# Values of pairs 4 to 15 from seven block products in place of eight, in an attention and feed-forward kernel

## What is computed

```python
def attention(x, Wq, bq, Wk, bk, Wv, bv, Wo, bo, gq, gk):
    q = rms_norm(x @ Wq + bq, gq)      # the norm runs over all 4096 columns
    k = rms_norm(x @ Wk + bk, gk)
    v = x @ Wv + bv                    # [1024 tokens, 4096]: 32 heads of 128
    attn = softmax(q @ k.T / sqrt(128))  # for each batch and head
    return (attn @ v) @ Wo + bo
x = x + layernorm(attention(layernorm(x), ...))
x = x + layernorm(ffn(layernorm(x), ...))
```

## Time and profile before

| | us |
|---|---|
| median of 3 runs | 1073.78 |
| lowest and highest | 1073.11, 1077.03 |
| span of the profiled execution | 1069.7 |

### The profile page before, as it was taken

One profiled execution on the slowest core, in us unless ns is written; L12 is line 12 of the kernel. 1 busy time (PEld: TensorE's weight loads), 2 busy tenths in 40 slices (PEclk: granted clock), 3 DMA queues, 4 the chain that ended last, 5 costly groups with the idle time before them and its releaser, 6 DMA issues.

```text
span 1069.7 us, 20038 instructions
## 1 busy us (share of the span) xinstructions
PE 1052.9 (98%) x5781; PEld 563.7 (53%) x5781; DVE 789.6 (74%) x1831; ACT 741.3 (69%) x1470; POOL 681.1 (64%) x597
## 2 busy tenths in 40 slices
PE   7999999999999999999999999999999999999997
PEld 4444444444445655555555555555555555555454
DVE  8767766666645887777777777777777777778887
ACT  4666766666656787676777767677776767777756
POOL 2667767676657476676666667666666766666713
PEclk9999999999999999999999999999999999999999
DMA  6688985656663679977676776767677676765702
GB/s 240 175 237 261 269 232 194 223 215 222 203 142 135 199 187 267 227 173 177 177 184 165 189 179 165 176 178 187 162 190 179 163 176 180 189 163 128 175 33 79
DMA packets 312072, 197.76 MB, mean 185 GB/s; under 512 B 275424, under 2 KB 279392, under 8 KB 312032
## 3 DMA queue, kind: packets, MB, share of 16 engines
q1 hardware_dynamic: 304400, 193.71, 65.5%
q10 hardware_dynamic: 7632, 3.57, 1.5%
HBM read 94.45 MB, written 35.68 MB: 122 GB/s over the span
## 4 chain that ended last, share of the span: by engine, by line
PE 91%; DVE 5%; ACT 2%; DMA 1%; issue 1%; SPq 0%; POOL 0%; DVEq 0%; ACTq 0%
PE ps L1236 30%; PE ps L1237 30%; PE ps L1238 30%; DMA wa_stage<-w_qk 1%; DVE pair_q L2061 1%; ACT ps L1031 0%; DVE ps L2047 0%; DVE stats L1630 0%; DMA pair_k<-pair_q 0%; ACT xh L1024 0%; ACT pair_q L1040 0%; PE ps L1348 0%; DVE y L2011 0%; DVE wa_lo L1735 0%; DVE y L2172 0%
## 5 line engine op out<-in xcount | busy, mean ns | idle before, releaser
L2047 DVE TENSOR_SCALAR_CACHE_REDUCE ps<-ps,score_down 128x512 f32<-128x512 f32 x256 | 177.5, 756 | 88.6 <-PE ps L1238 87.9
L2061 DVE SCALAR_TENSOR_TENSOR pair_q<-ps,row_inv,pair_q 128x512 f16<-128x512 f32 x256 | 174.5, 744 | 54.7 <-ACT pair_q L1040 54.6
L1031 ACT ACTIVATE ps<-ps,neg_max 128x512 f32<-128x512 f32 x256 | 168.2, 657 | 44.9 <-DVE ps L2047 44.9
L1236 PE MATMUL ps<-xh,wa_hi 128*128 128x512 f16 x512 | 194.3, 379 | 1.8 <-DVE wa_lo L1735 1.8
L1237 PE MATMUL ps<-xl,wa_hi 128*128 128x512 f16 x512 | 194.3, 379 | 0.0
L1238 PE MATMUL ps<-xh,wa_lo 128*128 128x512 f16 x512 | 194.3, 379 | 0.0
L1040 ACT ACTIVATE pair_q<-ps,row_inv 128x512 f16<-128x512 f32 x256 | 154.9, 688 | 21.5 <-DVE row_inv L2054 21.5
L758 POOL CAST oth<-o_t 128x512 f16<-128x512 f32 x62 | 37.8, 609 | 201.0 <-ACT o_t L1005 200.9
L664 POOL TENSOR_TENSOR acc<-acc,squares 128x512 f32<-128x512 f32 x120 | 151.1, 1281 | 1.7 <-ACT squares L882 1.7
L1237 PE MATMUL ps<-wv_lo,xh 128*128 128x256 f16 x512 | 139.7, 273 | 0.0
L1236 PE MATMUL ps<-wv_hi,xh 128*128 128x256 f16 x512 | 139.7, 273 | 0.0
(11 more groups left out here) (236 smaller groups left out, 2220.9 us busy)
## 6 DMA issues: line engine op xcount, KB each, us to landing
q_k_scratch<-qk_out SPq DMA_DIRECT2D x64, 512.0 KB, 3.9
qk_in<-q_k_scratch SPq DMA_DIRECT2D x64, 512.0 KB, 3.4
wa_stage<-w_qk SPq DMA_DIRECT2D x32, 512.0 KB, 4.8
u_stage<-w_vo SPq DMA_DIRECT2D x32, 512.0 KB, 5.5
wv_stage<-w_vo SPq DMA_DIRECT2D x16, 512.0 KB, 4.2
wo_stage<-w_vo SPq DMA_DIRECT2D x16, 512.0 KB, 4.4
qk_tops<-qk_top_scratch ACTq DMA_DIRECT2D x27, 128.0 KB, 4.2
y<-x SPq DMA_DIRECT2D x8, 256.0 KB, 5.4
```

What stands on the lines that cost most here:

```text
L1031: act.activation(ps[:, SCORE + i, :], ps[:, SCORE + i, :], ACT.Exp, bias=neg_max[:, sl, i:i + 1], scale=-1.0, accum_out=row_sum[:, sl, i:i ...
L1236: pe.matmul(outp, lhs[0], rhs[0], start=first, stop=False)
L2047: dve.tensor_scalar(ps[:, SCORE + i, :], ps[:, SCORE + i, :], score_down[:, sl, i:i + 1], None, ALU.mult, ALU.min, accum_out=neg_max[:, sl ...
L2061: dve.scalar_tensor_tensor(out=pair_q[:, 1, i, :], in0=ps[:, SCORE + i, :], scalar=row_inv[:, sl, i:i + 1], in1=pair_q[:, 0, i, :], op0=AL ...
```

## The change

For pairs 4 to 15, two pairs and two token tiles are taken as a 2 by 2 block product over the two halves of the 512 inner numbers: tiles t and t + 2, inner halves, and the two pairs' weights (256 columns each). Eight block products give the four results before; the new kernel forms seven (Strassen's scheme in Winograd's form: C, A, E, B, D, G, F), each two inner chunks of three matmuls of 256 columns. There are 24 groups of seven (`gi`): 6 double pairs, 4 tiles each (g). A group takes two steps. The step that begins one has products C and A behind `scores`, and E and B behind `attend`; the step that ends one has D and G behind `scores` and F behind `attend`. Steps 11 to 58 carry them. Steps 11 to 14 also still form values of pair 3 as before, into bank 7; steps 59 to 62 form none.

The partial sums share one bank: `WORK` and `ROOT` are the two halves of bank 6. ScalarE keeps a scaled C (`save_c`), copies ROOT over WORK three times a group (`copy_root`) and takes the second pair's high halves (`high_second`); VectorE adds for the first pair (`first_sums`) and takes the second pair's low halves (`low_second`); GpSimd splits the sums (`split_sums`). Sums of x are formed once on GpSimd in phase A (36 instructions); sums of weights, five for each double pair, on GpSimd, with seven high halves on ScalarE (`high_w`) and seven low halves on GpSimd (`low_w`). SP loads both pairs' weights at once (`load_both`) in place of `load_wv`. `wv` splits of pairs 4 to 15 fall away. The feed-forward weights, whose staging place the new loads use, are loaded and measured (`largest_of_base`) in pair 13 and no longer in pair 1. GpSimd's scaling of a weight has a second multiplication, by 1.0. Several semaphores are merged into `begun`.

```diff
-        X_UP, W_UP, QK_UP, P_UP = 2.0 ** 10, 2.0 ** 14, 2.0 ** 9, 2.0 ** 14
+        X_UP, W_UP, QK_UP, P_UP = 2.0 ** 9, 2.0 ** 14, 2.0 ** 9, 2.0 ** 14
...
+            def load_both(b):
+                for k, part in enumerate((first_w, second_w)):
+                    sp.dma_start(part, w_vo[bass.ds(2 * b + 4 + k, 1)].rearrange(
+                        "a p (h n) -> p (a h) n", h=2)).then_inc(f_loaded, 16)
...
+            with sp.Fori(1, FORMED) as c:
+                for j in range(8):
+                    step(2 * c + j // 4, j % 4)
+                    if j == 4:
+                        sp.wait_ge(w_low_ready, PARTS * c)
+                        load_both(c)
...
+            def form_x(dst, src, other, op):
+                pool.wait_ge(x_formed, x_forms[0])
+                x_forms[0] += 1
+                pool.tensor_tensor(dst, src, other, op).then_inc(x_formed, 1)
...
+            phase_a(1, high_a)
+            phase_a(2, low_a)
+            phase_a(3, both_halves)
+            phase_a(4, split_a)
+            phase_a(5, high_e)
+            phase_a(6, low_e)
+            phase_a(7, split_e)
+            phase_a(8, high_d)
+            phase_a(9, low_d)
+            phase_a(10, split_d)
+            phase_a(11, high_g)
+            phase_a(12, low_g)
+            phase_a(13, both_halves)
+            phase_a(14, split_g)
...
+            def low_w(b, k):
+                pool.wait_ge(w_high_ready, PARTS * b + k + 1)
+                pool.tensor_tensor(flat(w_low(k)), w_source(k), flat(w_high(k)),
+                                   ALU.subtract).then_inc(w_low_ready, 1)
...
+            def split_sums(g, gi):
+                tiles = slice(first_tile(g), first_tile(g) + 3, 2)
+                pool.wait_ge(q_sum_ready, 2 * gi + 2)
+                pool.sem_inc(begun, 1)
+                pool.tensor_copy(vh[:, tiles, :], v_s).then_inc(q_cast_ready, 1)
+                pool.wait_ge(q_cast_ready, gi + 1)
+                pool.tensor_tensor(vl[:, tiles, :], v_s, vh[:, tiles, :], ALU.subtract).then_inc(q_rest_ready, 1)
...
+            def building(c, j):
+                def some():
+                    if j == 0:
+                        form_g(c - 1)
+                    if j == 1:
+                        low_w(c - 1, W_C)
+                        low_w(c - 1, W_A)
+                    if j == 2:
+                        low_w(c - 1, W_E)
+                        low_w(c - 1, W_B)
+                    if j == 3:
+                        low_w(c - 1, W_D)
+                        low_w(c - 1, W_G)
+                    if j == 5:
+                        scale_first(c)
+                    if j == 6:
+                        form_c_and_b(c)
+                    if j == 7:
+                        form_e_and_f(c)
+                return some
...
+            def save_c(gi):
+                act.wait_ge(v_part, PARTS * gi + 2)
+                act.activation(c_s[:, :], WORK, ACT.Copy, scale=V_DOWN).then_inc(v_copied, 1)
+            def copy_root():
+                act.activation(WORK, ROOT, ACT.Copy).then_inc(v_copied, 1)
+            def high_second(g, gi, slot, last):
+                tile = first_tile(g) + 2 * last
+                act.wait_ge(v_part, PARTS * gi + (7 if last else 4))
+                act.activation(second_values(slot)[0][:, tile, :], WORK, ACT.Copy,
+                               scale=V_DOWN).then_inc(k_high_ready, 1)
+            def high_w(b, k):
+                act.activation(w_high(k).rearrange("p c n -> p (c n)"), w_source(k),
+                               ACT.Copy).then_inc(w_high_ready, 1)
...
-            def step(p, s, par, weights, value=True, prepare=True, between=None):
+            def step(p, s, par, weights, value=None, prepare=True, between=None, part=None, build=None):
                 n = 4 * p + s
                 sl = s % 2
+                begins, g, gi, slot = part or (None, None, None, None)
                 output(p, s)
                 if between:
                     between()
+                if begins is False:
+                    act.wait_ge(k_low_ready, 2 * gi + 1)
+                    copy_root()
                 for i in range(TB):
                     exponentials(n, sl, i)
+                if begins:
+                    save_c(gi)
                 if prepare:
                     high_k((s + 2) % 4, n + 2)
-                for i in range(TB):
+                if begins:
+                    act.wait_ge(v_copied, 4 * gi + 1)
+                    copy_root()
+                high_halves(n, sl, 0)
+                if begins is False:
+                    act.wait_ge(q_sum_ready, 2 * gi + 2)
+                    copy_root()
+                for i in range(1, TB):
                     high_halves(n, sl, i)
                 if value:
-                    evacuate_v(n + 2, 2 * ((s + 1) % 4), VB)
+                    bank, v = value
+                    evacuate_v(n + 2, 2 * ((s + 1) % 4), bank, v)
+                if part:
+                    high_second(g, gi, slot, not begins)
                 weights()
+                if build:
+                    build()
...
+            def product(k, g, half, first):
+                for c in range(2):
+                    x_hi, x_lo = x_operand(k, g, c)
+                    pe.matmul(half, x_hi, w_high(k)[:, c], start=first and c == 0, stop=False, skip_group_check=True)
+                    pe.matmul(half, x_hi, w_low(k)[:, c], start=False, stop=False, skip_group_check=True)
+                    ins = pe.matmul(half, x_lo, w_high(k)[:, c], start=False, stop=c == 1, skip_group_check=True)
+                ins.then_inc(v_part, 1)
+            def first_products(begins, g, gi, b):
+                if begins:
+                    if g == 0:
+                        pe.wait_ge(w_low_ready, PARTS * b + 2)
+                    if not isinstance(gi, int) or gi > 0:
+                        pe.wait_ge(q_sum_ready, 2 * gi)
+                        pe.wait_ge(k_low_ready, 2 * gi)
+                    product(W_C, g, WORK, True)
+                    product(W_A, g, ROOT, False)
+                else:
+                    if g == 0:
+                        pe.wait_ge(w_low_ready, PARTS * b + 6)
+                    pe.wait_ge(v_copied, 4 * gi + 3)
+                    product(W_D, g, ROOT, False)
+                    product(W_G, g, WORK, False)
+            def last_products(begins, g, gi, b):
+                if begins:
+                    if g == 0:
+                        pe.wait_ge(w_low_ready, PARTS * b + 4)
+                    pe.wait_ge(v_copied, 4 * gi + 2)
+                    product(W_E, g, ROOT, False)
+                    product(W_B, g, WORK, False)
+                else:
+                    if g == 0:
+                        pe.wait_ge(w_low_ready, PARTS * b + 7)
+                    pe.wait_ge(v_copied, 4 * gi + 4)
+                    product(W_F, g, WORK, False)
+            def step(p, s, par, value=None, part=None, b=None, v=(vh, vl), ready=None):
                 n = 4 * p + s
                 pe.wait_ge(qk_lo_ready, n + 1)
                 scores(n, s)
-                values(p, s, par, n)
+                if part:
+                    first_products(*part[0:3], b)
+                if value is not None:
+                    if value == OB:
+                        pe.wait_ge(o_t_ready, n - 1)
+                    values(p, s, par, n, value)
                 rows(p, s, par, n)
-                attend(n - 1, (s - 1) % 2, (s - 1) % 4 // 2)
+                if value == OB:
+                    pe.wait_ge(vl_ready, n + 2)
+                if ready:
+                    pe.wait_ge(*ready)
+                attend(n - 1, (s - 1) % 2, (s - 1) % 4 // 2, v=v)
+                if part:
+                    last_products(*part[0:3], b)
...
+            def first_sums(gi):
+                dve.wait_ge(v_part, PARTS * gi + 6)
+                dve.wait_ge(v_copied, 4 * gi + 3)
+                if not isinstance(gi, int) or gi > 0:
+                    dve.wait_ge(q_rest_ready, gi)
+                for k, half in enumerate((WORK, ROOT)):
+                    dve.scalar_tensor_tensor(out=v_s[:, k, :], in0=half, scalar=V_DOWN, in1=c_s[:, :],
+                                             op0=ALU.mult, op1=ALU.add).then_inc(q_sum_ready, 1)
+            def low_second(g, gi, slot, last):
+                tile = first_tile(g) + 2 * last
+                hi, lo = second_values(slot)
+                dve.wait_ge(k_high_ready, 2 * gi + last + 1)
+                dve.scalar_tensor_tensor(out=lo[:, tile, :], in0=WORK, scalar=V_DOWN, in1=hi[:, tile, :],
+                                         op0=ALU.mult, op1=ALU.subtract).then_inc(k_low_ready, 1)
...
+            def step(p, s, par, value=None, rows=True, down=True, to=None, part=None):
                 n = 4 * p + s
                 sl = s % 2
+                begins, g, gi, slot = part or (None, None, None, None)
                 maxima(n, sl)
                 if rows:
```

(9 more changed lines are left out.)

448 lines of the change are left out of this document (314 added, 134 removed).

## The result

| | before | after |
|---|---|---|
| median (4 runs each), us | 1073.44 | 1135.36 |
| lowest to highest, us | 1071.82 to 1077.03 | 1134.08 to 1135.93 |
| the profiled execution's own span, us | 1069.7 | 1133.3 |
| first `scores` of phase B starts, us | 350.06 | 357.10 |

The kernel after is slower: 1.0569 times the time of before, with a 95% interval of 1.0547 to 1.0590. The prediction was 1125 us in a range of 1090 to 1150.

What follows compares the result with a forecast made beforehand. TensorE was taken to bound phase B. Terms -15.8 + 44 + 6.6 + 6.4 + 7 + 3.5 = +51.7 us on the 1069.7 us span gave 1121.4, with 4.1 more 1125 us; range 1090 to 1150.

Steps and rivals of the forecast that it cites:

- the 4.1 us that it adds from span to median: Whole kernel: the median was taken to lie 4.1 us above the profiled span, turning 1121.4 us into 1125.
- 144 matmuls fewer: TensorE's value products: 1152 matmuls become 1008, at 0.109 us each, -15.8 us if TensorE stays full.
- steps 11 to 14, waits: At `attend`, waiting for VectorE's `split_v` while values are still formed: 4 x 1.6 = +6.4 us (3 to 9).
- steps 55 to 58, the same and the reductions: Waits for y and weight halves, plus feed-forward weight maxima in pairs 13 and 14 ahead of awaited maxima, +3.5 us.
- steps 59 to 62, waits: At `rows`, with no values or products left, TensorE waits for y: 4 x 1.75 = +7 us (6 to 8).
- phase A: 36 more GpSimd instructions of about 1.2 us over some 300 us, covered by idle time: no cost.
- The y term: At `rows`, TensorE waits 1.0 us per step for VectorE's addition to y: 44 steps, +44 us (17 to 75).
- The weight halves: ScalarE's `high_w` and GpSimd's `low_w` delay `otl`: +1.2 us per eight steps, 5.5 times, +6.6 us (0 to 15).
- The rival of a bound GpSimd: In five of eight steps `otl` comes 1 us later if GpSimd's forms cost more: +28 us, 1155 us; chance 0.12.
- half as dear again: On GpSimd, the new two-operation scaling and in-place sums might cost half as much again as the rows near them.
- rival of a clock below full speed in phase B: Phase B's 600 us at a mean granted clock of 0.9: matmuls some 60 us longer, 1185 us; chance 0.05.

Runs made afterwards that it cites:

- before_late: The kernel before with only the second half of each step's value matmuls moved from ahead of the output products to behind the attending product: 1169.58 us, ratio 1.0899.
- e_y: The kernel after with VectorE adding a step's output products to y at that step's own end, not behind the next step's maxima: 1127.85 us, ratio 1.0514.
- e_build: The kernel after with ScalarE taking o out ahead of the second lot's copy and weight halves, and GpSimd's weight remainders behind its split of o: 1151.45 us, ratio 1.0730.
- e_forms: The kernel after with GpSimd's last forms of x done a phase earlier in phase A: 1127.96 us, ratio 1.0511.
- e_unroll: The kernel after with the loops over four pairs written out on all five engines, so no jump back between steps 31 and 32: 1127.65 us, ratio 1.0510.
- e_ev: The kernel after with ScalarE's and VectorE's value copies of steps 11 to 14 placed earlier: 1129.52 us, ratio 1.0538.
- the kernel with all repairs: The kernel after with y added early, early value copies and x forms, loop written out, o taken out earlier, weight halves and remainders reordered: 1091.04 us, ratio 1.0172.

## Why the prediction was right, and where it was not

The sign and the range were right, and the forecast was 10 us low (12 us on the profiled span: the 4.1 us that it adds from span to median was 2.1 in the kernel after, which hid 2 us of the miss by luck). Its own steps:

| term | predicted, us | measured, us |
|---|---|---|
| 144 matmuls fewer | -15.8 | -15.7, of it 10.5 in steps 59 to 62 |
| steps 15 to 54, y and the weight halves | +46.0 (50.6 for 44 steps, 1.15 each) | +44.5, 1.11 each, without the jump back |
| steps 11 to 14, waits | +6.4 | +6.2 |
| steps 55 to 58, the same and the reductions | 4.6 + 3.5 | +6.7 |
| steps 59 to 62, waits | +7 | +9.0 |
| phase A | 0 | +7.0 |
| the jump back | not thought of | +6.0 |
| sum on the profiled span | +51.7 | +63.6 |

**The y term** came out as worked: 1.05 us in an ordinary step (1.0 predicted). The maxima start at T + 1.45 (predicted 1.45), the first addition ends and `rows` starts at T + 4.94 (predicted 4.9 to 5.0). That the maxima agree to 0.01 us is partly luck: ScalarE's copy starts at T + 0.20, not 0.37, and the maxima start 0.27 us after the scaling's end, for which the working had nothing. The two durations for which no row existed were half-size guesses: ScalarE's 128x256 copy 0.39 (0.40 guessed), VectorE's remainder 0.42 (0.43). before_late shows the mechanism without anything else of the change. What the prediction did not see is that this wait covers the one for `otl`: it may not be added back as a gain when y is repaired (e_y gave 18.3 us in steps 15 to 54 and 7.5 in all, where 44 were the term), and it is lengthened by anything put ahead of the second lot's copy (e_build).

**The weight halves** were over-valued: 1.2 us in eight steps predicted, about 0.5 measured (1.47 and 1.17 us in two steps where the others wait 1.05). In the table the two terms are one row, and the small excess of y fills part of the gap.

**Phase A** is the step that failed: "what costs nothing: 36 more GpSimd instructions, covered by idle time". The idle time was read as an average over slices; what counted was the order in the last phase, where three additions are waited for by everything. From 330 to 340 us GpSimd was busy 9.84 us of 10 already in before (9.92 in after), so there was no idle time left to cover them there, and its last additions start at 340.79, not 337.26. e_forms shows it: no instruction less, only earlier, and 6.5 of the 7.0 us are gone.

**The jump back** was missing. In before the loop's body is 8 steps and its turns show in no step; here it is 16 steps, and the turn costs 3.5 us where the clock stays up, and 6.0 in the profiled execution of the kernel after. e_unroll shows the 6.0. Whether the length of the body is the reason was not tested.

**Steps 59 to 62** lost 9.0 us, not 7: the term has four waits for y of 1.75, where there are three, of 6.9 us together, and 2.1 us in step 62, which has no `rows` to wait at and stands mainly at the transposes.

**The range.** The ends of the prediction's own terms add up to 1084 and 1169, not to "about 1090" and 1160; the measured time lies inside either pair.

**GpSimd's price.** The rival of a bound GpSimd rested on "half as dear again"; the two-operation scaling took 0.69 us, not 1.56, and the sums 1.27, as the rows near them. Of the scaling it had the sign of the price wrong, and `otl` was waited for 5.2 us in all (12.2 in e_y, where the wait for y no longer covers it).

**The clock.** The prediction's rival of a clock below full speed in phase B did not come. The windows from 500 to 700 and from 800 to 1010 us have 1.00, with a wait of about 1 us in nearly every step; in phase B it fell only behind the idle times of 1.7 and 2.6 us (at 719 and 727 us), and before it behind the 2.9 us at 345 us. In e_ev, with idle times of 2.0, 0.7 and 1.2 us around the same jump, it did not fall. The Trainium skill ("TensorE: Matmul & The Clock Gate", section "A second HAM failure mode: psum-queue depth-cycling") reports of another kernel that frequent short idles between groups of matmuls make the clock swing. These rows do not show it.

## What to carry over

Before moving work behind the last instruction of a step, follow the moved result through every in-order queue to what stands behind it: here 12 matmuls moved to the end brought TensorE 1.3 us earlier to the place where it needs y and VectorE's maxima 0.6 us later, with 0.9 us to spare. That cost each step 1.05 us, over three times the 0.33 us a step (24 matmuls in eight) that the saved products brought. When several waits end at one instruction, taking the longest away gains only its lead over the next, so undo them one by one *and* together. And "covered by idle time" has to be read in the phase where somebody waits for the engine's last instruction, not in the share of the span.

## What the runs showed of the hardware

- GpSimd's `tensor_scalar` on 128x512 with one operation takes 1.56 us, with two (the second times 1.0) 0.69 us. On 128x1024, with two, 1.12 us.
- A `tensor_scalar` of 128x5 on VectorE, from SBUF to SBUF, takes 0.22 us, and up to 1.33 us when a GpSimd instruction on SBUF is running. In the kernel with all repairs each of the 41 between 545 and 975 us ends within 0.04 us of the end of a GpSimd instruction. One row of before does not fit: 0.49 us at 992.11, over 0.8 us before the end of the GpSimd scaling that runs beside it. The Trainium skill ("SBUF — State Buffer", section "Who interferes with whom") says that `tensor_scalar` in a two-port mode and GpSimd take one shared pair of ports in turns, each for its whole instruction. The two pairs of rows shown under "All repairs together" agree, to 0.03 us; that this small instruction runs in such a mode is not shown by any run.
- A loop turn with 16 steps in its body left TensorE idle for 1.7 us, ScalarE for 3.0 and VectorE for 4.6; written out (e_unroll), the two steps around it are 6.0 us shorter.
- In the kernel after, TensorE's clock stayed at full speed through some 500 us with about 1 us of waiting in most steps of 11 us, and fell to half behind single idle times of 2.6 and 2.9 us. Behind 2.0 and 1.2 us in e_ev it stayed.
